# Two transformer layers on one core: the order in which an instruction's several waits are written

## What is computed

```python
# layer 0, per sample; mod = silu(condition) @ Wada + bada, cut in six
xm = layernorm(x) * (1 + sc_a) + sh_a
x  = x + gt_a * causal_attention(xm)            # scores * hd**-0.5, softmax, @ V, @ Wproj
xm = layernorm(x) * (1 + sc_m) + sh_m
x  = x + gt_m * (gelu(xm @ W1 + b1) @ W2 + b2)
# layer 1, per sample; sln is a layernorm with gamma and beta made from the condition
h   = sln(x)
att = softmax(q @ k.T) / sqrt(D)                # no mask
h1  = (att @ v) @ Wp.T + bp + x
out = sln(h1) + h1
```

## Time and profile before

| | |
|---|---|
| time of the runs | 1254.23 us median of 3 (1252.0 to 1255.34) |
| span of the profiled execution | 1249.3 us, from its first to its last instruction |
| PE, DVE, ACT, POOL busy | 94%, 68%, 54%, 22% of the span |
| granted TensorE clock | 0.984 of full speed on average |

### The profile page before, as it was taken

One profiled execution on the slowest core, in us unless ns is written; L12 is line 12 of the kernel. 1 busy time (PEld: TensorE's weight loads), 2 busy tenths in 40 slices (PEclk: granted clock), 3 DMA queues, 4 the chain that ended last, 5 costly groups with the idle time before them and its releaser, 6 DMA issues.

```text
span 1249.3 us, 18813 instructions
## 1 busy us (share of the span) xinstructions
PE 1168.6 (94%) x6604; PEld 591.7 (47%) x6604; DVE 850.9 (68%) x1779; ACT 678.2 (54%) x1346; POOL 279.0 (22%) x378
## 2 busy tenths in 40 slices
PE   7888989999899998999899999999989999999995
PEld 4434644464444644555344644446445553445332
DVE  4735498637886579836887378855788368754775
ACT  1272145656557465565555565564655656543673
POOL 1133022311332023311233013320243002310003
PEclk9898999999999999999999999999999999989998
DMA  5603031301432032500524024310425005200311
GB/s 177 192 2 102 2 112 41 111 12 65 117 87 69 19 109 74 135 4 19 149 52 118 2 73 109 100 57 18 113 69 137 1 2 162 39 17 25 91 33 42
DMA packets 59191, 89.36 MB, mean 72 GB/s; under 512 B 12914, under 2 KB 23762, under 8 KB 59098
## 3 DMA queue, kind: packets, MB, share of 16 engines
q1 hardware_dynamic: 58078, 87.35, 24.9%
q10 hardware_dynamic: 1020, 0.81, 0.2%
HBM read 24.41 MB, written 4.70 MB: 23 GB/s over the span
## 4 chain that ended last, share of the span: by engine, by line
PE 59%; DVE 20%; ACT 6%; SPq 5%; DMA 5%; issue 3%; POOL 1%; ACTq 0%; DVEq 0%; POOLq 0%
PE X L1034 13%; DVE MX L760 10%; PE OP L942 10%; PE X L1083 9%; PE X L1059 9%; PE SC L953 8%; PE X L972 8%; SPq L412 4%; ACT E L619 3%; DMA OC<-OE 2%; DVE STAT L769 2%; DMA QS<-NT 2%; DVE XN L812 1%; DVE XR L878 1%; DVE TMP L874 1%
## 5 line engine op out<-in xcount | busy, mean ns | idle before, releaser
L760 DVE TENSOR_REDUCE MX<-X 128x1 f32<-128x512 f32 (+3 forms) x1024 | 533.4, 581 | 187.6 <-PE X L975 100.0
L619 ACT ACTIVATE E<-SC 128x512 f32<-128x512 f32 (+3 forms) x1024 | 459.8, 525 | 323.6 <-PE SC L953 258.1
L972 PE MATMUL X<-KS,QS 96*128 96x512 bf16 (+3 forms) x1024 | 296.6, 346 | 10.7 <-DVE MX L760 6.4
L953 PE MATMUL SC<-QS,KS 99*128 99x512 bf16 (+3 forms) x1024 | 276.3, 342 | 24.9 <-ACT E L619 15.9
L942 PE MATMUL OP<-E,V 128*32 128x512 f32 (+3 forms) x2048 | 207.6, 523 | 6.2 <-ACT OE L634 5.4
L953 PEld LDWEIGHTS SC<-QS,KS 99*128 99x128 bf16 x1024 | 93.3, 97 | 176.0 <-ACT E L619 112.4
L972 PEld LDWEIGHTS X<-KS,QS 96*128 96x128 bf16 x1024 | 97.5, 98 | 160.5 <-DVE MX L760 51.2
L537 POOL TENSOR_SCALAR_AFFINE_SELECT E<-E 128x512 f32<-128x512 f32 x128 | 86.8, 680 | 252.4 <-ACT E L619 252.4
L1083 PE MATMUL X<-XT,W 128*128 128x512 f32 x256 | 123.8, 618 | 2.1 <-ACT XT L652 2.1
L1059 PE MATMUL X<-XT,WQKV 128*128 128x512 f32 x256 | 117.0, 602 | 1.5 <-ACT XT L652 1.5
L1034 PE MATMUL X<-W,HID 128*128 128x256 f32 x512 | 115.3, 380 | 0.4 <-ACT HID L672 0.4
(11 more groups left out here) (92 smaller groups left out, 920.4 us busy)
## 6 DMA issues: line engine op xcount, KB each, us to landing
QS<-PART SPq DMA_DIRECT2D x192, 128.0 KB, 2.4
KS<-PART SPq DMA_DIRECT2D x192, 128.0 KB, 2.5
OC<-OE SPq DMA_DIRECT2D x56, 128.0 KB, 3.9
RB<-recip_sums SPq DMA_DIRECT2D x56, 128.0 KB, 2.6
XIN<-in_x SPq DMA_DIRECT2D x8, 512.0 KB, 5.0
ROW<-row_vectors SPq DMA_DIRECT2D x8, 512.0 KB, 3.6
out<-OUT SPq DMA_DIRECT2D x7, 512.0 KB, 3.4
W<-in_w SPq DMA_DIRECT2D x2, 1024.0 KB, 6.7
```

Source lines behind the costliest of these rows:

```text
L619: a.activation(E[:, at["tick"].index() % 3, j, lo:T], SC[(at["head"].index() + j) % 3][:, lo:T], ACT.Exp, scale=HD ** -0.5 if layer == 0 e ...
L760: v.reduce_max(MX[:, qt, h:h + 1], X[at["bank"].index() % BANKS][:, 0:w], AX.X, negate=True)\
L953: t_.matmul(SC[(at["head"].index() + j) % 3][:, lo:T], KS[stacks(layer, b)][0:ALL_ROWS, h, kt * P:kt * P + P], QS[stacks(layer, b)][0:ALL_ ...
L972: ins = t_.matmul(bank[:, 0:w], QS[stacks(layer, b)][0:CUT_ROWS, h, qt * P:qt * P + P], KS[stacks(layer, b)][0:CUT_ROWS, h, 0:w], start=Tr ...
```

## The change

No instruction, buffer or semaphore is added or taken away, and every instruction still waits for the same values. Only the order in which the waits of one instruction are written is another, at these places (line numbers of the kernel before): ACT L619, L652, L665, L667, L672, L678, L685; DVE L836, L838, L858, L860, L874, L887, L896, L907; POOL L548, L563; PE L942 in layer 0, L1047, L1112. The core of the diff:

```diff
@@ ACT, exponentials (L619) @@
+                        wait(act, head_full, at["head"].at(1, j + 1))
                         if j == 0:
-
                             wait(act, pv_done, at["tick"].at(1, -2))
-                        wait(act, head_full, at["head"].at(1, j + 1))
@@ ACT and DVE, every dense chunk: the bank helper @@
                 def bank(k):
+                    wait(act, dense_full, c.at(1, k + 1))
                     if k == 0:
-
                         wait(act, dense_done, c.at())
-                    wait(act, dense_full, c.at(1, k + 1))
@@ DVE, proj0, down_1, down_3 (L874) @@
-                    wait(dve, row0_dma, at["rows0"].at(16))
-                    wait(dve, bias_pool, at["bias"].at())
-                    wait(dve, plus_pool, at["gain"].at())
...
+                        two, psum = slice(2 * tp, 2 * tp + 2), bank(n)
+                        if n == 0:
+                            wait(dve, row0_dma, at["rows0"].at(16))
+                            wait(dve, bias_pool, at["bias"].at())
+                            wait(dve, plus_pool, at["gain"].at())
@@ POOL, q0 and k0 (L563) @@
+                    wait(pool, dense_done, at["dense"].at(1, 2))
                     wait(pool, cut_low, c.at())
-
-                    wait(pool, dense_done, at["dense"].at(1, 2))
@@ PE, products of layer 0 (L942) @@
-                wait(pe, exp_done, at["step"].at(4, 4 * n + 4))
                 if layer == 0:
                     wait(pe, masked_pool, at["masked"].at(1, n + 1))
+                wait(pe, exp_done, at["step"].at(4, 4 * n + 4))
@@ PE, transposes of the maxima (L1112) @@
+                    wait(pe, max_pool, at["maxima"].at(4, 4))
                     psum = bank(0).bitcast(BF16)
-                    wait(pe, max_pool, at["maxima"].at(4, 4))
```

More of the change, by code:

```diff
@@ L657, in work @@
                     side = "qk".index(what[0])
-                    for half in range(2):
-                        wait(act, stack_dma[0][half], at["stack0"].at(192))
-                        wait(act, stack_dma[1][half], at["stack1"].at(192))
                     for t in range(2):
-                        part = PART[:, side, 0, t, :]
+                        part, psum = PART[:, side, 0, t, :], bank(t)
+                        if t == 0:
+                            for half in range(2):
+                                wait(act, stack_dma[0][half], at["stack0"].at(192))
+                                wait(act, stack_dma[1][half], at["stack1"].at(192))
                         if what[1] == "0":
-                            ins = a.activation(part, bank(t)[:], ACT.Copy)
+                            ins = a.activation(part, psum[:], ACT.Copy)
                         else:
-                            ins = a.activation(part, bank(t)[:], ACT.Identity,
+                            ins = a.activation(part, psum[:], ACT.Identity,
                                                bias=BQK1[:, 2 * side + t:2 * side + t + 1])
@@ L785, in bank @@
                 def bank(k):
+                    wait(dve, dense_full, c.at(1, k + 1))
                     if k == 0:
                         wait(dve, dense_done, c.at())
-                    wait(dve, dense_full, c.at(1, k + 1))
                     if what in ("down_1", "down_3"):
@@ L829, in work @@
                     part = PART[:, side, :, :, :]
-                    wait(dve, cut_low, at["low"].at())
-                    wait(dve, dense_done, c.at())
                     for t in range(2):
                         wait(dve, high_act, at["high"].at(1, t + 1))
+                        if t == 0:
+                            wait(dve, cut_low, at["low"].at())
                         if what[1] == "0":
@@ L863, in work @@
                 elif what in ("proj0", "down_1", "down_3"):
-                    wait(dve, row0_dma, at["rows0"].at(16))
-                    wait(dve, bias_pool, at["bias"].at())
-                    wait(dve, plus_pool, at["gain"].at())
-                    if what == "down_1":
-                        wait(dve, hold_pool, at["hold"].at())
                     gate, dst = (0, XR) if what == "proj0" else (2, R1)
@@ L872, in work @@
                     for n, tp in enumerate(pairs):
-                        two = slice(2 * tp, 2 * tp + 2)
-                        v.tensor_tensor(TMP[:, two, :], bank(n)[:].rearrange("p (t d) -> p t d", d=D),
+                        two, psum = slice(2 * tp, 2 * tp + 2), bank(n)
[3 more added lines that the diff above has]
+                            wait(dve, plus_pool, at["gain"].at())
+                            if what == "down_1":
+                                wait(dve, hold_pool, at["hold"].at())
+                        v.tensor_tensor(TMP[:, two, :], psum[:].rearrange("p (t d) -> p t d", d=D),
                                         ROW0[:, gate:gate + 1, :].to_broadcast([P, 2, D]), ALU.mult)\
@@ L883, in work @@
                 elif what == "proj1":
-                    wait(dve, plus_pool, at["gain"].at())
-                    wait(dve, hold_pool, at["hold"].at())
                     for tp in range(2):
-                        v.tensor_tensor(TMP[:, 2 * tp:2 * tp + 2, :], bank(tp)[:].rearrange("p (t d) -> p t d", d=D),
+                        psum = bank(tp)
+                        if tp == 0:
+                            wait(dve, plus_pool, at["gain"].at())
+                            wait(dve, hold_pool, at["hold"].at())
+                        v.tensor_tensor(TMP[:, 2 * tp:2 * tp + 2, :], psum[:].rearrange("p (t d) -> p t d", d=D),
                                         RH[:, 2 * tp:2 * tp + 2, :], ALU.add).then_inc(dense_done, 1)
@@ L904, in work @@
                 elif what in ("scale0", "scale1"):
+                    wait(dve, spread_dma, at["sums"].at(64))
                     wait(dve, compact_dma, at["pack"].at(64))
-                    wait(dve, spread_dma, at["sums"].at(64))
                     v.tensor_tensor(OC[:], OC[:], RB[:], ALU.mult).then_inc(scaled_dve, 1)
@@ L1042, in work @@
                     for ft in range(KT):
+                        if ft == 0:
+                            wait(pe, norm_dve, at["norm"].at(4, -3))
                         psum = bank(ft)
                         for t in range(TT):
-                            if ft == 0:
+                            if ft == 0 and t > 0:
                                 wait(pe, norm_dve, at["norm"].at(4, t - 3))
```

## The result

| | before | the change |
|---|---|---|
| time, median of 6 runs each, side by side | 1254.01 us (1252.0 to 1258.25) | 1242.47 us (1241.4 to 1245.84) |
| ratio, 95% interval | | 0.9915 [0.9892, 0.9937] |
| span of the profiled execution | 1249.3 us | 1244.1 us |

The account below looks back on a forecast made before the run. The prediction took the kernel as PE-bound, PE busy 94% of the span. Terms 2.8 + 1.4 + 0.8 + 0.1 - 0.5 = 4.6 us, less 0.2 for neighbouring paths, gave a 4.4 us gain: 1249.8 us, range 1245.0 to 1253.5.

Parts of the forecast that it names:

- the 7 that were to be a sign of error: PE's gaps, 80.7 us over the span: a fall of more than 7 us would show the prediction wrong.
- the table loads: ACT's table loads run before PE's result: priced at 0; as rival, gain 9 us, 1245 us, chance 0.10.
- The slower rival: POOL's L565 and DVE's L878 or similar collide, 1.39 us each, 9.7 us for seven: 1259.5 us, chance 0.05.
- places on the chain x difference: Gain summed as places on the chain of waits times the start difference: 0.06 ACT, 0.10 DVE, 0.09 us PE.
- exponentials, L619: First of ACT's four exponentials per step: about 33 chain places at 0.06 us; 0.3 us lost where pv_done comes last.
- ACT's dense steps: ACT: 7 chain places ahead of L672 and some 6 ahead of L652, L678 and L685, at 0.06 us each.
- L1112's own start: PE's L1112 waiting for POOL: 9 chain places at 0.09 us, 0.8 us.
- DVE: L874 about 11 chain places, L896 and L907 3 more, at 0.10 us: 1.4 us.
- products, POOL: PE's products L942 in layer 0 and POOL's L563 and L548: nothing gained.
- other back-losses and paths: About 0.2 us lost for L896 and L838, and 0.2 us taken off for neighbouring paths.
- The anchor: Profiled span 1249.3 us less 4.4, plus 4.9 us between span and median of the runs: 1249.8 us.
- PE is the busiest engine: Skill rule to improve the busiest engine first, PE at 94%: no gain, 1254.2 us; chance inside the covered case's 0.27.

Follow-up runs that it names:

- e9: The kernel before with only ACT's dense steps (L652, L665, L667, L672, L678, L685) in the change's wait order: 1249.52 us, ratio 0.997.
- e16: The kernel before with ACT's dense steps in the change's order and the output's store issued only after QS<-NT has landed: 1249.11 us, ratio 0.9965.
- the late store: The kernel before with one more wait on SP, so the store out<-OUT is issued only after QS<-NT has landed: 1250.46 us, ratio 0.9994.
- e7: The kernel before with only PE's transposes of the maxima (L1112) in the change's wait order: 1250.32 us, ratio 0.9972.
- e14: The change, with small RS<-OE issued behind the four OC<-OE instead of ahead, in pack1 of the five repeated passes: 1266.35 us, ratio 1.0095.

## Why the prediction was wrong

**Right: the mechanism and its sizes per start.** The pieces of 0.02 and 0.04 stand where they were expected, PE's busy time stays near 1168 us, PE's idle time fell by 5.4 and 6.3 us, under the 7 that were to be a sign of error, and POOL, the products and the table loads are worth nothing measurable. The timeline of ACT in the change shows a load right behind the activation ahead of it, and one behind the freed buffer instead of behind PE's result, and PE's pair of stops, 0.98 and 1.19 us, has become one of 2.24, which is the prediction's "PE would only stand there longer". Timelines of ACT and of PE:

```profile
531.87 1.28 ACT L669 ACT_TABLE_LOAD   x1
...
535.32 1.28 ACT L617 ACT_TABLE_LOAD   x1 [0.60 <-PE OP L941]
...
157.41 0.28 PE L971 MATMUL X<-KS,QS 96*128 96x256 bf16 x1 [2.24 <-DVE MX L757]
```

The slower rival did not come either: five collisions, as before, the second of them in the timeline of DVE:

```profile
518.11 2.06 DVE L875 TENSOR_TENSOR XR<-XR,TMP 128x512 f32<-128x512 f32 x1
```

**Wrong: "places on the chain x difference" as the whole sum.** The step that failed is the one that let the change act only through the starts. It left out without a reason what a DMA issue that moves does to another queue's transfer, and the clock. The 9 us at an equal clock are, by the runs:

| term | predicted | measured |
|---|---|---|
| exponentials, L619 | 2.0 less 0.3 | 2.4 +- 1.3 |
| ACT's dense steps | 0.8 | 1.7 and 1.5, both +- 1.5 (e9 less 1.4, e16 less the late store's 1.8) |
| L1112's own start | 0.8 | 1.4 +- 1.4 (e7, less 1.8) |
| DVE | 1.4 | 0.8 +- 1.5 |
| products, POOL | 0 | 0.4 and 0.2, both +- 1.0 |
| QS<-NT ahead of the store | not seen | 1.8 +- 0.9 |
| sum | 4.4 (with 0.1 for L1047, less 0.4 for other back-losses and paths) | 8.6, with an error of about 3 (the terms' errors taken as independent); the whole change 8.8 +- 1.0 and 9.5 +- 1.3 |

The missing term stood in the waits of before as 2.4 us in 6 stops of the same length, and in the chain as a transfer of 3.49 us where most others of its kind take 2.6 to 2.75. (Five more, issued beside the transfers OC<-OE, take 2.90 to 4.03 us in before and 3.31 to 4.14 in the change, which left them as they were; whether they cost anything was not tried.) I looked at what the changed instructions wait for and not at what they issue: L685 is followed by a DMA issue, and its rank against another queue's was open by a tenth of a microsecond.

**Mis-sized: the starts.** Without the transfer 7.0 us of the 8.8 are left (+- 1.4) where 4.4 were taken. Part of the 4.4 is itself counted too high. Followed once over the whole span, the chain of before has a piece of 0.08 to 0.17 us ahead of L619 21 times (33 in the prediction), a piece of 0.12 ahead of L874 7 times (11), one ahead of L896 and L907 4 times (3), and the 0.14 ahead of L1112 6 times (9). With the 14 other places on ACT the prediction's own rule gives 2.1 + 1.1 + 0.5 + 0.1 - 0.5 = 3.3 us, before its 0.2 for neighbouring paths. So places on the chain give about half of what was measured. Which term is short can't be told: every row of the table lies within its error of the price. PE's own stops are a second way to count. L1112 has 15 of them, and 15 x 0.09 = 1.35 us; L619 has 38, and 38 x 0.06 = 2.3, and PE's stops for it fell by 2.1 net. Both fit the measured 1.4 and 2.4, but so do the 0.8 and 1.7 of the prediction, and by them too the sum stays under 7. What carries the rest stays open.

**Not in the sum: the granted clock.** The rest of the 11 us, 0.0024 x 970 = 2.3 us, goes with the clock. It is higher in the change, and in none of the parts is it clearly so (0.9808 to 0.984). A stretch of the change and the same place of before show what a low stretch is; in both PE has just stood for OE (start:end, length, engines, clock, and so on), the change first:

```profile
616.00:620.00 4.00, 3.09 (x17) 0.76 (x18) 1.35 (x3) 1.21 (x4) 0.00 (x0) 0.57 0.43 131
```

```profile
619.00:623.00 4.00, 3.87 (x30) 1.41 (x34) 2.55 (x5) 1.92 (x7) 0.63 (x1) 1.00 0.52 148
```

The profile of before happened to have no such drop between 200 and 1090 us, those of its parts had up to three, the two of the change two and one. That long stops bring drops is shown by e14; that the change's many slightly shorter stops make them rarer would fit, but the stops for OE, beside which its own drops stand, aren't shorter in it (5.5 us in 5 stops, before 5.4 in 6), no run took it apart, and it stays open.

**The anchor** held by luck of its own: the prediction called the 4.9 us between span and median "what lies around the span". That is 1.7 us; the other 3 are that the profiled run was better than the median. The sum would have been the same. Whoever takes the difference of the two profiled spans (5.2 us) for the gain sees less than half of it.

That PE is the busiest engine doesn't speak against the change, as the prediction took it to: what the change shortens is PE's own idle time, from starts on the engines that PE waits for.

## What to carry to other kernels

Let an instruction carry the wait that comes last, on PE, DVE and ACT alike, and take a count of places on the chain as no more than a rough price: here the starts gave about twice of it. Look behind every start that moves for a DMA issue, and in the waits for a row of equal short stops behind a transfer that takes longer than its kind: its place against the other queue's transfer can be won or lost by a tenth of a microsecond. And before a small transfer is moved behind its neighbours, look at how long its reader waits now: 0.16 us is no slack.

## What was not expected of the hardware

- A lead of 0.28 us between two issues on two queues gives a landing of 3.42 to 3.53 us, one of 0.33 mostly 3.25 and once 2.60, and one of 0.35 or more 2.63 to 2.74, the same as with no other transfer near (2.64 to 2.79).
- The delay grows with what stands between the decisive wait and the instruction: 0.02 us on ACT where the instruction carries it, 0.08 with one piece of ACTq, 0.16 with two (OE, above).
- Stops of PE of 3.35 to 3.71 us had 6.8 us at half clock behind them all six times (in the two kernels with RS<-OE behind its neighbours), stops of 1.98 to 2.23 us 3.4 us twice and 6.8 twice. Beside stops of 0.3 to 1.8 us there were 3.4 us of it in some executions, 6.8 in two, and none in others.
